# Softmax attentions: values placed between first-pass scores, and the next batch's first maxima taken beside the last group

## The reference

```
q = (x @ Wq.T).reshape(B, T, h, dh).transpose(0, 2, 1, 3)      # k, v alike
att = jnp.einsum('bhqd,bhkd->bhqk', q, k) / jnp.sqrt(jnp.float32(dh))
p = jax.nn.softmax(att, axis=-1)
out = jnp.einsum('bhqk,bhkd->bhqd', p, v)
out = out.transpose(0, 2, 1, 3).reshape(B, T, D)
return out @ Wo.T
```

```
absorbed_k = (W_q @ W_uk).reshape(H, DH, L)
c_kv = _layernorm(jnp.einsum('bsd,ld->bsl', x, Wd_kv), gamma, beta)
q = x.reshape(B, S, H, DH)
tmp = jnp.einsum('bshd,hdl->bhsl', q, absorbed_k)
scores = jnp.einsum('bhsl,btl->bhst', tmp, c_kv) / np.sqrt(DH)
scores = jnp.where(mask[None, None], scores, -jnp.inf)
attn = jax.nn.softmax(scores, axis=-1)
v_full = jnp.einsum('btl,dl->btd', c_kv, W_uv).reshape(B, S_full, H, DH)
```

## Time and profile before

| | us |
|---|---|
| median of 3 runs | 3280.82 |
| the runs | 3280.82, 3280.75, 3301.81 |
| profiled execution | 3300.27 |
| its span, first to last instruction | 3298.5 |
| mean granted TensorE clock | 0.904 |
| layer 1, loop over 4 batches | 474.43 |
| layer 7, loop over 4 batches | 483.96 |

### The profile page before, as it was taken

One profiled execution on the slowest core, in us unless ns is written; L12 is line 12 of the kernel. 1 busy time (PEld: TensorE's weight loads), 2 busy tenths in 40 slices (PEclk: granted clock), 3 DMA queues, 4 the chain that ended last, 5 costly groups with the idle time before them and its releaser, 6 DMA issues. The chain is left out here.

```text
span 3298.5 us, 46216 instructions
## 1 busy us (share of the span) xinstructions
PE 2929.7 (89%) x15538; PEld 1983.0 (60%) x15538; DVE 1659.9 (50%) x4515; ACT 822.9 (25%) x1344; POOL 975.2 (30%) x1089
## 2 busy tenths in 40 slices
PE   7999999999999999999979999999998458888972
PEld 3434447787556555788857777777776324444452
DVE  4454455666555656366644333333335545544545
ACT  2242244443101011344422222222220002212200
POOL 0000006666444435576621222222221002112100
PEclk9998899999999999999989999999997658777775
DMA  3000002000000000100000000000000000000000
GB/s 132 1 0 0 0 0 97 0 0 0 0 1 0 0 0 0 77 0 0 0 13 14 14 1 14 14 14 14 1 1 18 5 0 1 0 0 0 0 0 26
DMA packets 6281, 37.88 MB, mean 11 GB/s; under 512 B 272, under 2 KB 4368, under 8 KB 4496
## 3 DMA queue, kind: packets, MB, share of 16 engines
q1 hardware_dynamic: 6160, 36.34, 2.8%
HBM read 34.24 MB, written 2.10 MB: 11 GB/s over the span
## 5 line engine op out<-in xcount | busy, mean ns | idle before, releaser
L669 PE MATMUL banks<-back 32*128 32x512 f32 (+3 forms) x1024 | 375.2, 656 | 31.5 <-DVE back L834 10.1
L364 PE MATMUL banks<-moe_parts 128*128 128x512 f32 x1536 | 368.9, 396 | 13.7 <-POOL moe_parts L444 8.2
L364 PEld LDWEIGHTS banks<-moe_parts 128*128 128x128 f32 x1536 | 288.4, 191 | 76.7 <-issue 18.5
L1445 PE MATMUL banks<-lin_parts 128*128 128x512 f32 x1152 | 308.0, 413 | 18.8 <-DVE lin_parts L1696 15.5
L801 ACT ACTIVATE back<-banks 128x1024 f32<-128x1024 f32 (+3 forms) x256 | 213.6, 862 | 292.8 <-PE banks L687 291.8
L1631 DVE TENSOR_TENSOR ffn_pack<-banks,back 128x512 f32<-128x512 f32 x128 | 88.5, 691 | 353.4 <-PE banks L1458 353.3
L1445 PEld LDWEIGHTS banks<-lin_parts 128*128 128x128 f32 x1152 | 213.8, 195 | 67.2 <-issue 21.0
L687 PE MATMUL banks<-back 32*128 32x512 f32 (+3 forms) x1024 | 242.6, 619 | 6.7 <-DVE back L863 2.9
L669 PEld LDWEIGHTS banks<-back 32*128 32x128 f32 x1024 | 143.1, 219 | 153.9 <-DVE back L838 59.4
L1761 POOL TENSOR_TENSOR ffn_pack<-ffn_pack 128x256 f32<-128x256 f32 x112 | 83.0, 741 | 499.6 <-ACT ffn_pack L1594 499.6
L838 DVE TENSOR_REDUCE back<-banks 128x1 f32<-128x512 f32 x256 | 165.0, 686 | 113.7 <-PE banks L669 110.9
(11 more groups left out here) (224 smaller groups left out, 5251.4 us busy)
## 6 DMA issues: line engine op xcount, KB each, us to landing
back<-p_raw SPq DMA_DIRECT2D x8, 1024.0 KB, 4.8
back<-p SPq DMA_DIRECT2D x1, 7696.0 KB, 21.3
ffn_pack<-ffn SPq DMA_DIRECT2D x1, 6144.0 KB, 26.8
back<-p SPq DMA_DIRECT2D x1, 5152.0 KB, 15.1
back<-p SPq DMA_DIRECT2D x2, 1792.0 KB, 8.1
out<-x SPq DMA_DIRECT2D x1, 2048.0 KB, 7.5
x<-x_in SPq DMA_DIRECT2D x1, 1536.0 KB, 12.7
small_pack<-small SPq DMA_DIRECT2D x1, 619.0 KB, 4.9
```

The source lines that it names most:

```text
L364: mm = nc.tensor.matmul(bank[:], up[:, n % 2, a, which, kd, :], xp[:, b, kd, :], start=((a, b, kd) == (0, 0, 0)), stop=((a, b, kd) == (1, ...
L669: nc.tensor.matmul(bank[:, 0:n], qs[head_rows[j], hg, qi * P:(qi + 1) * P], ks[head_rows[j], hg, 0:n], start=True, stop=True).then_inc(D.f ...
L1445: mm = nc.tensor.matmul(bank[:], wp[:, a, m, kd, r * P:(r + 1) * P], xp[:, b, x, kd, :], start=((a, x, kd) == (0, 0, 0)), stop=((a, x, kd) ...
```

## The change

On all engines the same order is changed:

- The first pass of group 0 is no longer at the head of the batch. The loop computes the maxima of group `(hg + 1) % 4` beside group `hg`, so beside group 3 those of the next batch's group 0. For batch 0 they are computed once, in the block before the loop, which ends with `turn_max` and `put_max`. The loop of the last batch also computes maxima for a batch that doesn't follow.
- At the head of a batch only `v_tiles` stays, and TensorE waits for the last copy of v.
- Within a key tile the order becomes T0 T1 S3, values of the key tile before, S0 T2 T3 S1, the extras (`beside`), S2. `MAX_ORDER` is (3, 0, 1, 2). On VectorE the extras stand ahead of the fourth maximum, the layernorm step behind it.
- `qk` is issued at the end of each group for the group two ahead, ahead of `turn_max` and the last values; the two projections in the tail are gone.
- `turn_xn` and the whole latent work move from group 3 to group 2.

```diff
-MAX_ORDER = (2, 3, 0, 1)
+MAX_ORDER = (3, 0, 1, 2)
...
@@ set-up block, TensorE @@
+            pe.wait_ge(A.free.s, A.released(0, "k", 0))
+            for qi in range(NT):
+                for j in MAX_ORDER:
+                    scores(pe, 0, 0, qi, j)
+            turn_max(pe, 0, 0, 1)
+            pe.wait_ge(A.free.s, A.released(0, "k", 1))
+            pe.wait_ge(D.free.s, D.released(0, "turn", 0))
...
@@ loop, TensorE @@
-                scores(0, 0, MAX_ORDER)
-                v_tiles(V_TILES[0])
-                scores(0, 1, MAX_ORDER)
-                v_tiles(V_TILES[1])
-                scores(0, 2, MAX_ORDER)
-                v_tiles(V_TILES[2])
-                scores(0, 3, MAX_ORDER)
-                turn_max(0)
-                qk(pe, it, 2)
...
+                def beside(hg, kt):
+                    if hg and kt == 1:
+                        denominators(hg - 1)
+                    if hg and kt == 2:
+                        turn_reciprocals(hg - 1)
+                    if hg == 2 and kt == 0:
+                        turn_xn(nc, c, pe, it)
+                    if hg == 2 and kt == 1:
+                        pe.wait_ge(D.free.s, D.released(it, "xt", 1))
+                        w.project_latent(pe, it)
+                    if hg == 2 and kt == NT - 1:
+                        w.turn_latent(pe, it)
+
+                for tiles in V_TILES:
+                    v_tiles(tiles)
+                pe.wait_ge(D.free.s, D.released(it, "v", V_TILES[-1]))
                 pe.wait_ge(A.free.s, A.all_free(it))
                 for hg in range(HG):
+                    after = (hg + 1) % HG
                     for kt in range(NT):
+                        scores_t(hg, kt, 0)
+                        if hg and kt == 0:
+                            pe.wait_ge(A.free.s, A.released(it, "k", after))
+                        scores(pe, it, after, kt, MAX_ORDER[0])
                         if kt:
                             values(hg, kt - 1)
+                        scores(pe, it, after, kt, MAX_ORDER[1])
+                        scores_t(hg, kt, 1)
+                        scores(pe, it, after, kt, MAX_ORDER[2])
+                        beside(hg, kt)
+                        scores(pe, it, after, kt, MAX_ORDER[3])
+                    qk(pe, it, (hg + 2) % HG)
+                    turn_max(pe, it, after, hg + 1)
+                    values(hg, NT - 1)
                     if hg + 1 < HG:
-                        turn_max(hg + 1)
-                    values(hg, NT - 1)
-                    if hg + 3 < HG:
-                        qk(pe, it, hg + 3)
-                qk(pe, it, 0)
+                        pe.wait_ge(D.free.s, D.released(it, "turn", after))
                 denominators(HG - 1)
...
-                pe.wait_ge(A.free.s, A.released(it, "y", NT - 1))
-                qk(pe, it, 1)
+                pe.wait_ge(A.free.s, A.released(it, "k", 1))
+                pe.wait_ge(D.free.s, D.released(it, "turn", 0))
...
@@ loop, VectorE @@
+                for tiles in V_TILES:
+                    keep_v(tiles)
                 for hg in range(HG):
+                    after = (hg + 1) % HG
                     for kt in range(NT):
+                        for j in MAX_ORDER[:-1]:
+                            maximum(dve, it, after, kt, j)
+                        beside(hg, kt)
+                        maximum(dve, it, after, kt, MAX_ORDER[-1])
                         if norm:
                             norm.pop(0)()
...
+                    negate_max(dve, it, after)
+                    put_max(dve, it, after)
                     dve.wait_ge(O.full.s, O.may_read(it))
```

More of the change, by code:

```diff
@@ L67, in take, with open @@
         self.banks = banks
-    def open(self, uses):
-        assert uses % len(self.banks) == 0
+    def open(self, uses, whole=True):
+        assert not whole or uses % len(self.banks) == 0
         self.full.open(uses)
@@ L589, in keep_qk, with scores, maximum, negate_max @@
             .then_inc(A.free.s, 2)
+    def scores(pe, it, hg, qi, j):
+        n = (qi + 1) * P if causal else T
+        pe.wait_ge(D.free.s, D.may_fill(it))
+        bank = D.fill("max", hg, qi, j)
+        nc.tensor.matmul(bank[:, 0:n], qs[head_rows[j], hg, qi * P:(qi + 1) * P], ks[head_rows[j], hg, 0:n],
+                         start=True, stop=True).then_inc(D.full.s, 1)
+    def maximum(dve, it, hg, qi, j):
+        n = (qi + 1) * P if causal else T
+        dve.wait_ge(D.full.s, D.may_read(it))
+        bank = D.read("max", hg, qi, j)
+        if causal:
+            turn = (D.r - 1) % len(D.banks)
+            apart(nc, c, 4 + turn)
+            ins = nc.vector.tensor_tensor_reduce(
+                w.scratch[:, turn, 0:n], bank[:, 0:n], w.mask[:, T - n:T], 1.0, -3e38, ALU.add, ALU.max,
+                mx[:, qi, j:j + 1])
+        else:
+            ins = nc.vector.tensor_reduce(mx[:, qi, j:j + 1], bank[:], AX, ALU.max)
+        ins.then_inc(D.free.s, 1)
+    def negate_max(dve, it, hg):
+        dve.wait_ge(D.free.s, D.released(it, "max", hg, NT - 1, MAX_ORDER[-1]))
+        nc.vector.tensor_scalar(slots[:, :, :, 0], mx, -1.0, None, ALU.mult).then_inc(c.max_ready.s, 1)
+    def turn_max(pe, it, hg, k):
+        pe.wait_ge(c.max_ready.s, c.max_ready.at(it, k))
+        pe.wait_ge(D.free.s, D.may_fill(it))
+        bank = D.fill("turn", hg)
+        for i in range(NT):
+            mm = nc.tensor.transpose(bank[:, i * P:(i + 1) * P], mp[:, i, :], c.ident[:])
+        mm.then_inc(D.full.s, 1)
+    def put_max(dve, it, hg):
+        dve.wait_ge(D.full.s, D.may_read(it))
+        bank = D.read("turn", hg)
+        nc.vector.tensor_tensor(qs[:, hg, :], qs[:, hg, :], bank[:], ALU.add).then_inc(D.free.s, 1)
     A.open(4)
-    D.open(w.extra_uses)
+    D.open(w.extra_uses + max_uses, whole=False)
     c.first_step.open(w.links)
+    c.max_ready.open(1)
     if causal:
@@ L621, in _ @@
             w.keep_latent(dve, 0)
+            for qi in range(NT):
+                for j in MAX_ORDER:
+                    maximum(dve, 0, 0, qi, j)
+            negate_max(dve, 0, 0)
+            put_max(dve, 0, 0)
         @block.gpsimd
@@ L635, in _ @@
             loads(sp)
-    for k in (A, D, c.first_step):
+    for k in (A, D, c.first_step, c.max_ready):
         k.close(1)
@@ L661, in v_tiles @@
                     mm.then_inc(D.full.s, 1)
[L663 to L678, removed]
                 def scores_t(hg, kt, pair):
                     q0 = kt * P if causal else 0
+                    pe.wait_ge(A.free.s, A.may_fill(it, 2))
                     for j in (2 * pair, 2 * pair + 1):
-                        if j % 2 == 0:
-                            pe.wait_ge(A.free.s, A.may_fill(it, 2))
                         bank = A.fill("s", hg, kt, j)
@@ L688, in scores_t @@
                                               qs[head_rows[j], hg, q0:T], start=True, stop=True)
[L689 to L690 removed]
+                    mm.then_inc(A.full.s, 2)
                 def values(hg, kt):
@@ L822, in keep_v @@
                         .then_inc(D.free.s, 1)
[L824 to L840, removed]
-                        dve.wait_ge(D.free.s, D.released(it, "max", hg, qi, MAX_ORDER[-1]))
-                        nc.vector.tensor_scalar(slots[:, :, :, 0], mx, -1.0, None, ALU.mult)\
-                            .then_inc(c.max_ready.s, 1)
                 def invert(hg):
```

73 lines of the change are left out of this document (19 added, 54 removed).

## The result

The changed kernel takes 3193.15 us (median of 4 runs, 3191.56 to 3196.5), the kernel before 3291.23 us beside it (4 runs, 3280.75 to 3301.81). The ratio is 0.970, 95% interval 0.966 to 0.975: 98 us, or 3%, faster. Forecast were 3214 us, and 67 us less than the median of before. The profiled executions took 3191.56 (span 3188.7) and 3300.27 (span 3298.5), 109 us apart. Where one run of a kernel stands far above its others at a lower granted clock (one of eleven in experiment 3, 3565.53 us at 0.779), it is left out of the median.

What follows compares the result with a forecast made beforehand. TensorE's loop of matmul, maximum, matmul, values was taken as the bound, 4.02 us a key tile. Layer 1's -42 and layer 7's -25 made -67 off the median 3280.82: 3214 us, range 3160 to 3270.

Steps and rivals of the forecast that it cites:

- the likeliest case: Whole program: the forecast itself holds, a gain of 40 to 95 us, 3186 to 3241 us; chance 0.53.
- Rival (b): Key tile: the new order shortens it to 3.1 us, some 57 us more gain, 3157 us; chance 0.09.
- Part 1: Key tile order: values between the scores leave the period at 4.02 us; costed at 0.
- the same loop, rotated: Key tile: in the new order a wait for a maximum still stands ahead of the values, period again 4.02 us.
- Part 2: Layer 1's groups laid out new: 20.6, 22.0, 23.3 and 22.0 us, group 3 becoming like group 1.
- Parts 3 and 4: Layer 1's batch head without first pass, only values tiles, 4.8 us; its tail without two projections, 10.6 us for 18.9.
- it is done in time: Head of a batch: VectorE adds the residual first, then copies v, without holding TensorE up.
- The allowance of 14 us a batch: Layer 7: cost of 1.2 GHz stretches above the 96.2 us walked at full clock, bounds 0 and 28.
- rival (a): Layer 7: idle TensorE lowers the clock, 8.4 us per slow group; chance 0.17 for gain cut to 0–35, 0.05 for loss.
- Rival (d): Layer 7: the clock gets better, full clock giving 14 x 4 us less, 3158 us; chance 0.10.
- rival (c): Scores: four-abreast running fails, or each extra tiling mode change costs about 0.5 us, +32, 3246 us; chance 0.06.
- The count of 64: Groups: denominators and reciprocals between scores add two tiling mode changes a group, 64 in all, costed at nothing.

Runs made afterwards that it cites:

- experiment 3: Changed kernel with group 0's first pass back at the head of each batch and no scores beside group 3: 3316.4 us, median of ten runs.
- run 2: Changed kernel in which each maximum of layer 1 reads 256 of its 512 columns, every matmul the same: 3170.68 us, one run.
- run 1: Changed kernel with the key tile order of before (T0 T1 S2 S3 T2 T3 S0 S1, values, extras): 3206.07 us.
- Run 9: Changed kernel with v copied by ScalarE instead of VectorE at the head of a batch: 3185.02 us, ratio 0.964 to the kernel before.
- run 7: Changed kernel with four unread 128x512 matmuls in layer 7's group 2, where TensorE waits for the latent chain: 3168.77 us.
- run 8: Kernel before with four unread matmuls in layer 7's group 3, where TensorE waits for the latent chain: 3285.59 us, ratio 0.995.
- run 4: Changed kernel with denominators and turned reciprocals straight behind the values instead of between first-pass scores: 3209.96 us, one run.

## Why the prediction was right, and where it was off

The measured 3193 lies in the range, and in the likeliest case (3186 to 3241). That case was counted from 3281; from the 3291 measured beside the changed kernel the gain is 98, just past its 95.

**What bounds the loop.** Right. The period is matmul, maximum, matmul, values in either order; 3.95 for 4.02, and run 2 moved it by exactly one maximum. Rival (b), a key tile of 3.1 us, is refuted.

**Part 1 at nothing.** Off. The order is worth 17.5 us in layer 1 and costs 6.0 in layer 7 (run 1). The step that failed is "the same loop, rotated": I compared the plain key tiles in the middle of a group and left out its head, where the old order puts eight maxima in a row on VectorE; the heads are 2.1 of the 3.5 us a batch. The other 1.4 stood in my own walk, 4.7 against 5.0 for a key tile with denominators (measured 4.55 against 5.00), and were put at nothing. The last 3.7 are moments at half clock. The wait of the values for the mask in layer 7 I had named and then not charged to the order.

**Part 2, the groups.** The walk gave 20.6, 22.0, 23.3, 22.0; measured are 19.7, 21.2, 22.1, 20.9. Each term was sized too large by 0.8 to 1.2, a little at each hand-over: first values 4.1 for 3.8, then 4.7 for 4.55 twice, and so on. Four a batch is 16 us in layer 1 and carries most of the miss there. Group 3 did become a group 1.

**Parts 3 and 4.** In layer 1 v took 4.3 (4.8) and the tail 10.3 (10.6); batches are 98.5 apart for 103.3, and the set-up pass 17.3 for 18. The layer gave -61 for -42. In layer 7 the head of a batch took 4.95 for 3.0. The step that failed is "it is done in time": VectorE ends the residual adds in time and then stands 2.6 us before it begins the copies, for no wait that the profile shows. Run 9 shows that the copies are what TensorE waits for, and not why they are late. Part 4's own terms give 10.5, not 10.6.

**Layer 7.** -42 for -25. A batch took 107.7 for 110.2, the first pass in the set-up block about 13 us for 17. Group 2 took 34.2 at clock 0.75; the 30.8 was a walk at full clock. Group 3 took 17.6 for 17.8. The wait behind the latent chain was 4.4 for "some 5".

**The clock.** The allowance of 14 us a batch above the walk at full clock (its terms, 8.4, 4.2 and 2, make 14.6) is of the right size: 107.7 less 96.2 is 11.5, of which the head's missed 2 are none of the clock's. As the walk ran too long in layer 1, the clock's true share may be larger. Its mechanism, rival (a), is real (run 7: 5.2 a batch from one wait) but small. It didn't turn the sign because the old kernel paid it too: the same filler gives 4.0 a batch there (run 8). Rival (d), layer 7 at full clock, came in part: 0.83, from 0.74. The whole-program clock rose from 0.904 to 0.929.

**The drain by tiling changes, rival (c).** No run shows a price: four abreast stayed, and with the extras back at the values no key tile got shorter, and the ones with denominators got 0.39 longer where the lost cover was to cost 0.5 (run 4). The count of 64 was too high: group 0 has no extras, so it is 2 changes in 24 groups, 48.

**The sum.** 67 was forecast; 109 came between the profiled executions and 98 between the medians. Of the 42 us between 67 and 109, layer 1 has 19 (16 of them its groups), layer 7 has 17, and 6 lie outside the stretches that were forecast. The medians are 11 closer than the profiled executions, since that of before lies 9 us above its median. Most terms were too long; only the head of layer 7's batch was too short. The forecast was right on where the gain lies, and its sum came out a third too small.

## What to carry to other kernels

Work that stands alone at the head of an iteration, here 16 matmuls waiting for maxima one after another, costs its own length and the lower clock; beside the last part of the iteration before, it was worth 107 us over eight batches, and reordering the loop body 12 (17.5 less 6.0). When an order is compared, walk the first turns of the loop and the queues of the other engines there, not only the steady period. A long wait on TensorE should be priced with the clock of the work behind it: here waits of 3.7 and 4.4 us cost 4.0 and 5.2 us a batch beyond their own length. If it can't be removed, matmuls that nobody reads, placed in it, are worth trying.

## What the hardware showed that was not expected

Four unread 128x512 matmuls in a wait (3.70 us) shortened the program by 24 us; cutting the same wait into one of 1.5 and one of 1.1 us left the clock at 0.50. First-pass scores that run one after another stay at 0.50 although TensorE is busy for 18.3 of 20.1 us. At a change of batch in layer 7 VectorE stood 2.6 us between two instructions with no wait to show for it, and TensorE waited for it. And the kernel before, unchanged, spread over 3280.6 to 3308.0 in 13 runs of one set with its clock from 0.912 down to 0.902, so its time and the clock it is granted go together; the changed kernel's four runs lie within 5 us.
